# The last attention's softmax sums: folded to 128x8, inverted there, read back broadcast, and the product moved to GpSimd, with a new order of steps

## The reference

```python
q = (x @ Wq).reshape(b, n, 16, 64).transpose(0, 2, 1, 3) * 64 ** -0.5
kv = jnp.concatenate([jnp.broadcast_to(null_kv, (b, 1, 64)), x @ Wkv], axis=1)
sim = jnp.einsum('bhid,bjd->bhij', q, kv)
attn = softmax(where(causal_mask, mask_value, sim))
out = jnp.einsum('bhij,bjd->bhid', attn, kv)
return out.transpose(0, 2, 1, 3).reshape(b, n, 1024) @ Wout
```

## Time and profile before

| | us |
|---|---|
| median of 3 runs | 2005.79 (2002.66 to 2008.48) |
| profiled execution | 2003.36 |
| its span, first to last instruction | 2001.0 |
| last attention in it, jobs and close | about 1430 to 1930 |

### The profile page before, as it was taken

One profiled execution on the slowest core, in us unless ns is written; L12 is line 12 of the kernel. 1 busy time (PEld: TensorE's weight loads), 2 busy tenths in 40 slices (PEclk: granted clock), 3 DMA queues, 4 the chain that ended last, 5 costly groups with the idle time before them and its releaser, 6 DMA issues.

```text
span 2001.0 us, 31764 instructions
## 1 busy us (share of the span) xinstructions
PE 1849.8 (92%) x9960; PEld 1272.3 (64%) x9960; DVE 1399.3 (70%) x3825; ACT 964.6 (48%) x2008; POOL 1225.7 (61%) x1600
## 2 busy tenths in 40 slices
PE   5999999999895999999999999998999999899985
PEld 4566666666694666666676567887556665455554
DVE  8898888888344776766666456455788888776733
ACT  2544445545454455455455435444444444455443
POOL 1766788888553566776777700012467676799744
PEclk8999999999997899999999999999899999999998
DMA  5224233322344334344344120001322222222243
GB/s 149 67 70 114 68 94 95 79 57 60 89 142 114 84 84 98 86 110 95 88 101 98 42 88 22 1 13 30 82 57 57 65 68 60 65 77 70 56 117 98
DMA packets 125968, 155.57 MB, mean 78 GB/s; under 512 B 21880, under 2 KB 66200, under 8 KB 125544
## 3 DMA queue, kind: packets, MB, share of 16 engines
q1 hardware_dynamic: 121704, 145.42, 29.5%
q0 software_dynamic: 4096, 8.12, 1.2%
HBM read 47.84 MB, written 17.40 MB: 33 GB/s over the span
## 4 chain that ended last, share of the span: by engine, by line
PE 60%; DVE 14%; POOL 9%; issue 8%; ACT 3%; DMA 3%; SPq 3%; POOLq 0%; DVEq 0%; ACTq 0%
PE P L858 59%; POOL acc L1639 3%; POOL yd L1656 3%; DVE mx L2019 2%; DVE P L2030 2%; SPq L1760 1%; POOL acc L1636 1%; DMA qA<-hq 1%; POOL pr L1617 1%; POOL xg L1647 1%; DVE rd L2078 1%; DVE P L2077 1%; DVE z L2084 1%; PE P L957 1%; DVE mx L2040 0%
## 5 line engine op out<-in xcount | busy, mean ns | idle before, releaser
L1639 POOL TENSOR_TENSOR acc<-acc,pr 128x512 f32<-128x512 f32 (+3 forms) x768 | 677.3, 904 | 87.3 <-ACT pr L1398 63.0
L1398 ACT ACTIVATE pr<-P 128x512 f32<-128x512 f32 (+1 forms) x768 | 396.9, 568 | 331.4 <-PE P L858 288.0
L858 PE MATMUL P<-qA,kA 128*128 128x512 f32 (+2 forms) x1024 | 392.9, 387 | 17.1 <-ACT pr L1398 11.1
L858 PE MATMUL P<-pr,vt 128*64 128x512 f32 (+3 forms) x2304 | 403.3, 491 | 4.7 <-POOL pr L1617 4.5
L858 PE MATMUL P<-qB,kB 128*128 128x512 f32 (+2 forms) x1024 | 367.8, 365 | 0.0
L858 PE MATMUL P<-kA,qA 128*128 128x512 f32 (+2 forms) x1152 | 318.2, 376 | 30.5 <-DMA qA<-hq 9.3
L1617 POOL TENSOR_SCALAR_AFFINE_SELECT pr<-pr 128x256 f32<-128x256 f32 x384 | 156.5, 408 | 272.6 <-ACT pr L1398 215.7
L858 PEld LDWEIGHTS P<-pr,vt 128*64 128x64 f32 x2304 | 155.2, 137 | 217.3 <-issue 178.7
L2019 DVE TENSOR_REDUCE mx<-P 128x1 f32<-128x512 f32 x384 | 241.6, 683 | 30.8 <-PE P L858 29.0
L858 PEld LDWEIGHTS P<-qA,kA 128*128 128x128 f32 x1024 | 195.1, 191 | 102.8 <-ACT pr L1398 48.5
L858 PEld LDWEIGHTS P<-kA,qA 128*128 128x128 f32 x1152 | 193.7, 195 | 102.1 <-issue 25.8
(11 more groups left out here) (350 smaller groups left out, 2766.0 us busy)
## 6 DMA issues: line engine op xcount, KB each, us to landing
qA<-hq SPq DMA_DIRECT2D x384, 128.0 KB
kA<-stage SPq DMA_DIRECT2D x158, 128.0 KB, 2.3
qB<-qB SPq DMA_DIRECT2D x96, 128.0 KB, 2.5
kB<-stage SPq DMA_DIRECT2D x79, 128.0 KB
nr<-null_share SPq DMA_DIRECT2D x64, 128.0 KB, 3.0
yd<-in_c_zero SPq DMA_DIRECT2D x32, 128.0 KB, 2.7
w<-in_L_W SPq DMA_DIRECT2D x16, 256.0 KB, 5.0
xg<-xg SPq DMA_DIRECT2D x24, 129.0 KB
```

What stands on the lines that cost most here:

```text
L858: return P.matmul(out, lhs, rhs, start=start, stop=stop)
L1398: S.activation(a.pr[slot][:, r, 512 - wide:512], m.bank[b][:, 512 - wide:512], AF.Exp, scale=0.125).then_inc(s.free[b], 1)
L1639: G.tensor_tensor(acc[:, sl], acc[:, sl], pt[:, sl], ALU.add).then_inc(s.acc, 1)
```

## The change

Nothing changes in layers 0 to 2 but the way an index is written. In the last attention, for all chunks but the two of the last job (`at_once` is true for those, and for the other layers):

- The sums go another way. ACT copies the closed sums out of the bank into `rd` (`close`), which frees the bank. SP folds two partitions of `rd`, 1024 numbers, to 128x8 in `rc` (`fold`). DVE adds the null key's share, which now comes back as 128x8 in `nl` by one transfer, and takes the reciprocal, both at 128x8 (`recip`). SP writes the result to DRAM (`spread`) and reads it back broadcast over 64 partitions for each head into `rb` (`cast`). ACT copies the bank of `pv` to `z` (`zraw`), and POOL multiplies `z` by `rb` (`div`).
- `dsum`, the two ACT steps, the three DVE steps and the two broadcasts of `nr` go away there.
- The two heads' additions to `acc` become one instruction of twice the width.
- `STEPS[3]` is rewritten. `mxe` gets a step `X` of its own, later than `mxc`. A job has 16 `+`. The step `C1` stands behind the second `S` as before; `C0` moves from behind the seventh `S` to behind the ninth. The steps left over at the end are issued behind the last job.

```diff
-HELD = {"close": "div",  "q": "qlo", "k": "klo"}
+def at_once(L, b, p):
+    return L != 3 or (b, p) == (1, 7)
...
-    3: ("k0' + q0' S q0 k0 V3 + k0\" + R1 q0\" S + C1 + k1 + + S D1 S V3 + M2 + S M0 S k1' q1' q1 + S M1 + C0 "
-        "v0 + V k1\" + R0 q1\" D0 + v1 + M6 S + M3 M4 S M5 S M8 S S + M7 O1 O0 M9 +")}
+    3: ("q0 k0' + + k0 k1 q0' S k0\" V3 + R1 S q0\" + v0 F1 C1 S S + M1 M0 k1' S q1' q1 S + W1 + Z1 B1 q1\" M2 "
+        "I1 + + S v1 k1\" + V4 O0' M5 S + + F0 X0 M3 D1 S M6 C0 + R0 + M4 S M9 W0 I0 V4 + + M8 Z0 S M7 S D0 X1 "
+        "O1 B0")}
...
 ScalarE
+            elif kind == "close" and not at_once(*k[0:3]):
+                S.copy(a.rd[:], ps[:]).then_inc(s.free[b], 1)
+            elif kind == "zraw":
+                S.copy(a.z[pl.chunk(*k) % 4][:], m.bank[b][:]).then_inc(s.free[b], 1)
...
 GpSimd
-                        G.tensor_tensor(acc[:, sl], acc[:, sl], pt[:, sl], ALU.add).then_inc(s.acc, 1)
+                        G.tensor_tensor(acc[:, :, sl], acc[:, :, sl], pt[:, :, sl], ALU.add).then_inc(s.acc, 1)
+            elif kind == "div" and not at_once(*k[0:3]):
+                w.wait_ge(s.cast, 16 * od.nth("cast", *k))
+                G.tensor_tensor(z[:], z[:], a.rb[n][:], ALU.mult).then_inc(s.div, 1)
...
 SyncE
+                    src = nd[i].rearrange("i n -> (i n)").rearrange("(p e) -> p e", e=8)
+                    Y.dma_start(m.A[3].nl[i % 4][:], src).then_inc(s.n_in[i % 2], 16)
+            elif kind == "fold":
+                w.wait_ge(*pl.emptied("close", *k))
+                Y.dma_start(a.rc[n][:], a.rd[0:128:64, :].rearrange("r (p e) -> r p e", e=8)).then_inc(s.fold, 16)
+            elif kind == "spread":
+                w.wait_ge(s.recip, od.nth("recip", *k))
+                Y.dma_start(sd[...].rearrange("(p e) -> p e", e=8), m.A[k[0]].rc[n][:]).then_inc(s.spread, 16)
+            elif kind == "cast":
+                w.wait_ge(s.spread, 16 * od.nth("spread", *k))
+                Y.dma_start(a.rb[n][:], src).then_inc(s.cast, 16)
...
 VectorE
+            elif kind == "recip":
+                w.wait_ge(s.fold, 16 * od.nth("fold", *k))
+                    chain(V.tensor_tensor(a.rc[n][:], a.rc[n][:], a.nl[i % 4][:], ALU.add))
+                V.reciprocal(a.rc[n][:], a.rc[n][:]).then_inc(s.recip, 1)
```

More of the change, by code:

```diff
@@ L146, in add @@
                 turn.append(b)
-                if kind in HELD and len(got) == n - 1:
+                if kind in HELD and len(got) == n - 1 and (kind != "close" or at_once(*item[1:4])):
                     self.held[b] = (HELD[kind],) + item[1:]
@@ L196 @@
 SCORED = [(0, kt) for kt in range(4)] + [(1, kt) for kt in range(8)]
+SHARES_OUT = {"C": "close", "F": "fold", "I": "recip", "W": "spread", "B": "cast", "Z": "zraw", "D": "div", "O": "out"}
 STEPS = {
@@ L283, in step @@
             od.extend(project(L, "k", jobs[j + 1][0], keys(j + 1)[0], n)["'\"".find(what[-1]) + 1])
+        elif what[0] == "X" and at < 15:
+            od.add("mxe", L, *jobs[at + 1], int(what[1]))
         elif what[0] == "R":
@@ L289, in step, with finish @@
                     od.add("nrd", L, *jobs[at], n)
-        elif what[0] == "C" and done:
-            od.add("close", *done)
-            if L == 3:
-                od.add("dsum", *done)
-        elif what[0] == "D" and done:
-            od.add("div", *done)
-        elif what[0] == "O" and done:
-            if done[2] % 2:
-                if L == 3 and done == (3, 0, 1, 0):
-                    od.add("nbias", L)
-                od.add("out", *done)
+        elif what[0] in SHARES_OUT and done:
+            finish(SHARES_OUT[what[0]], done)
+    def finish(kind, done):
+        b, p = done[1:3]
+        if kind == "out":
+            if p % 2:
+                if done == (3, 0, 1, 0):
+                    od.add("nbias", 3)
+                od.add("out", *done)
+        elif not at_once(L, b, p):
+            od.add(kind, *done)
+        elif kind == "close":
+            od.extend([(x,) + done for x in ("close", "dsum", "yinv") if L == 3 or x != "dsum"])
+        elif kind == "div":
+            od.add("div", *done)
     scored = []
@@ L334, in attention_order @@
     od.extend([("pv", *k) for k in scored])
-    od.extend([(k, L, 1, 7, 1) for k in ("close", "dsum", "div", "out") if L == 3 or k != "dsum"])
+    left = [(L, *jobs[j], c) for j in range(13, 16) for c in range(2)]
+    for kind in SHARES_OUT.values():
+        for done in left:
+            if (kind,) + done not in od.place:
+                finish(kind, done)
     for items in behind:
@@ L609, in attention @@
         a.rd = sb(stack, "rd", [128, 512])
+        if L == 3:
+            a.rb = [sb(stack, f"rb{i}", [128, 512]) for i in range(2)]
+            a.rc = [sb(stack, f"rc{i}", [128, 8]) for i in range(2)]
         a.mx = [sb(stack, f"mx{i}", [128, 72]) for i in range(2)]
@@ L716, in signals @@
     s.w_hi, s.root, s.xn_a, s.x_hi = one("w_hi"), one("root"), one("xn_a"), one("x_hi")
-    s.q_hi, s.k_hi, s.inv = one("q_hi"), one("k_hi"), one("inv")
+    s.q_hi, s.k_hi, s.inv, s.recip, s.div = one("q_hi"), one("k_hi"), one("inv"), one("recip"), one("div")
+    s.fold, s.spread, s.cast = one("fold"), one("spread"), one("cast")
     s.rt_wh, s.rt_exp, s.xs, s.c_act, s.silu = one("rt_wh"), one("rt_exp"), one("xs"), one("c_act"), one("silu")
@@ L759, in __init__ @@
                 self.normed |= {(it[1], g): n for g in range(lo // 4, hi // 4)}
+        self.casts = [it[1:] for it in od.items if it[0] == "cast"]
+        self.closes = [it[1:] for it in od.items if it[0] == "close"]
+        self.n_div = {}
+        for it in od.items:
+            if it[0] == "div" and not at_once(*it[1:4]):
+                self.n_div[it[1:]] = len(self.n_div) + 1
         self.adds, n = {}, 0
@@ L784, in weighed, with cast_slot, close_before @@
     def weighed(self, L, b, p, c):
+        if not at_once(L, b, p):
+            return self.s.div, self.n_div[L, b, p, c]
         return self.emptied("pv", L, b, p, c, 0)
+    def cast_slot(self, a, *k):
+        casts = [x for x in self.casts if x[0] == k[0]]
+        i, n = casts.index(k), len(a.rb)
+        return i % n, casts[i - n] if i >= n else None
+    def close_before(self, *k):
+        i = self.closes.index(k)
+        return self.closes[i - 1] if i and self.closes[i - 1][0] == k[0] else None
     def keys_copied(self, n, second=False):
```

87 lines of the change are left out of this document (62 added, 25 removed).

## The result

The changed kernel took 2020.38 us in the median of 4 runs (2017.39 to 2024.72), against 2004.85 for the kernel before in the same comparison (2002.66 to 2008.48): a ratio of 1.008, 95% interval 1.0057 to 1.0103. It is slower, by 0.8%, and lies above the range that was predicted. Its profiled execution took 2017.39 us, with a span of 2015.6.

What follows compares the result with a forecast made beforehand. Bisection jobs were taken as bound by PE, scatter jobs by POOL, with PE idle 34.5 us in 500. From 2003.36: first routing job -2, bisection -2.6, slots -3, scatters +1, end 0, together -6.6, so 1997 us; range 1980 to 2012.

Steps and rivals of the forecast that it cites:

- The prediction's part on SP and the DMAs: New transfer chain from the sums' close to the product: 10 to 13 us with queueing, counted as costing nothing.
- Scatter jobs: Last-attention jobs with scatters, bound by POOL: stay at about 32.9 us, but fill 4.0 jobs rather than 3.6; counted +1.
- rival 2: Scatter jobs: merged additions save nothing, POOL waits about 1 us at one product of each pair; 2011 us, chance 0.14.
- First routing job: First last-attention job with routing, 35.5 us, DVE as its bound: -2 of PE's 3.3 us idle.
- Bisection jobs: Six last-attention jobs, 30.8 us each, bound by PE: half of their 5.2 us idle goes, -2.6.
- Slots and scatters together: Two jobs around the slots, stalled behind closings on DVE: -3 with a little clock; the jobs with scatters: +1.
- `X`: Exp of the null key's score, moved later: takes away ACT's 110.6 us of waits, counted at nothing beyond the idle shares.
- The number of `+`: 16 for 18 in a job: 8 scatters rather than 9, over 4.0 jobs rather than 3.6, +2 us.
- the middle course: DVE's relief in the last attention, allowing for longer waits at small steps: about 1 to 3 us a job.
- rival 3: Bisection jobs: DVE's small SBUF steps each wait for a merged POOL addition; about 2018 us, chance 0.09.
- The end: Last job, closed the old way: one POOL product more (+1.3), merged additions (-1.5), output moved; counted 0.
- Rival 1: Last attention: PE loses almost no time outside the scatter jobs and scatters cost nothing more; 1983 us, chance 0.18.

Runs made afterwards that it cites:

- e1: The changed kernel with the broadcast `cast` issued as two transfers, one a head with 64 partitions each, in place of one: 1986.2 us, ratio 0.9893.
- e12: e1 with the product by 1/sum on GpSimd in jobs up to the tenth and on VectorE from the tenth on: 1978.0 us, ratio 0.9851.
- e9: The kernel before with only the exp of the null key's score (`X`) moved to a later step of its own: 2009.83 us, ratio 1.0006.
- e6: e1 with the exp of the null key's score (`X`) put back directly behind the comparison: 2005.36 us, ratio 1.0003.
- e10: The kernel before with `X` moved later and the two heads' additions merged, old order and closing otherwise: 1994.48 us, ratio 0.9912.
- e4: The kernel before with only the two heads' additions in the last attention merged into one instruction: 2002.9 us, ratio 0.9967.
- e7: e1 with the two heads' additions as two instructions again: 1993.89 us, ratio 0.9943.
- e11: e1 with 18 `+` in a job, as in the kernel before, in place of 16: 2019.71 us, ratio 1.0045.
- e3: The kernel before with its two broadcasts of `nr` made into one transfer of outermost dimension 2: 2011.34 us, ratio 1.0016.

## Why the prediction was wrong

**The broadcast, the step that failed.** The prediction's part on SP and the DMAs took `cast` at 3.0 to 3.3 us, from two broadcasts of 64 partitions and a load of 256 KB, and went from size alone. It measured 8.24 and 8.62 where it stood on the chain. The rows it leant on were of broadcasts with an outermost dimension of 64. The line that builds `src`, the first one of e1's diff, has a 2 there and stood in the changed kernel to be read. With 3.0 us the chain came to 10 to 13, and "there POOL may stand for 0 to 3 us" was then closed with "POOL is behind PE, so the cast has landed. Nothing, then." With 5 more, 25 products wait for 2.9 each, and copies and scatters come late with them. This one term is what separates the changed kernel from e1: 34 us. The small transfers of the chain were over-priced, but that did not help: writing the inverted sums to DRAM landed in 1.4 us in the median, for 2.0 to 3.0.

**Without that step** the forecast of 1997 would still have been 11 us too high: e1 takes 1986.2 (by its ratio, on the 2004.85 of the first comparison, 1983). So the whole size, the right sign included, hung on one transfer. The terms, by e1:

- Scatter jobs: forecast four at 32 to 33, in e1 33.2 each over three (99.68 / 3), and the neighbours that hold the rest at 30.5 and 29.8. Right. So rival 2 had the place and the engine. But its 1 us of waiting for each pair is not there in e1 (5.1 us in all), and in the changed kernel it is far more, in nearly all jobs, and from a cause that the rival did not name.
- First routing job: forecast -2, in e1 -2.1. Right.
- Bisection jobs: forecast -2.6 over six, "bound by PE", with 5.2 us in all to win. In e1 they win 9.2 (175.5 for 184.7). The step that failed is the floor: PE's busy time was read as work that can't shrink. The six jobs of e1:

```profile
1491.25:1666.74 175.49, 173.80 (x950) 113.92 (x951) 131.88 (x434) 87.97 (x195) 137.80 (x127) 1.00 0.30 70
```

  PE is busy 173.8 us for 179.5 before, at the full clock in both. A part of that may be moved work, as these jobs hold 96 items of the bisection in place of 108. From the last layer's weights to the end of the span the work is the same, 3243 matmuls recorded, and busy time shrinks there too, in the kernel before and then in e1:

```profile
1307.64:2001.00 693.36, 621.61 (x3243) 411.73 (x3241) 487.45 (x1413) 320.34 (x700) 427.47 (x551) 0.96 0.25 66
```
```profile
1311.02:1985.50 674.48, 611.03 (x3243) 412.59 (x3241) 424.35 (x1353) 318.01 (x700) 440.69 (x405) 0.95 0.27 68
```

  The profile models the ends of matmuls, so a stretch with matmuls queued in it reads as busy. In the bisection jobs the idle time was no ceiling; over the whole layer the best run, e12, wins 28.7 us (693.4 - 664.7), less than the 34.5 of idle time.
- Slots and scatters together: forecast -3 and +1. In e1 -8.8 (219.1 for 227.9 in the marks 8 to 15). No run takes the two apart. The two jobs at 33.8 and 38.0, at a clock of 0.95 and 0.91, have no like in e1: the jobs around its slots take 29.2 and 30.5 at the full clock. The clock's share, counted as "a little", is by an estimate at most 5 of these 12 us (0.05 x 33.8 + 0.09 x 38.0); the rest is not taken apart.
- `X`, counted "at nothing": right in the old order (e9, 1.0006), and worth 19 us of medians in the new one (e6 against e1, 2005.36 - 1986.2). In the old order it is worth 8 us as soon as the additions are merged (e10 against e4). So ACT's 110.6 us of waiting cost nothing only while something else was late; that this was GpSimd's additions is argued, not shown.
- The merged additions: an instruction of 1024 takes 2380 ns for two of 1281, as worked out, and the saving of 1.5 a job was bounded well. Yet alone they are worth 6 us (e4), and 8 in e1 (e7). Over 16 jobs 1.5 would be 24; it shows where POOL binds.
- The number of `+`: treated as a question of how many jobs hold scatters, +2 us for having fewer. Measured, 18 in place of 16 cost 33.5 us in the new order (e11), at the two places tried. Fewer is far better here, for a reason that was not foreseen; the term had the wrong sign and was too small by a factor of ten and more.
- VectorE. The groups of the changed kernel in 1430 to 1930 (busy, mean ns, idle before), with POOL's:

```profile
L1701 POOL TENSOR_TENSOR acc<-acc,pr 128x1024 f32<-128x1024 f32 x47 | 111.9, 2380 | 20.2 <-ACT pr L1444 17.4
...
L1707 POOL TENSOR_TENSOR z<-z,rb 128x512 f32<-128x512 f32 x30 | 38.3, 1275 | 72.5 <-DMA rb<-sum_share 72.4
...
L2132 DVE TENSOR_TENSOR mx<-mx,sn 128x8 fp32r<-128x8 f32 x29 | 22.7, 784 | 1.0
...
L2133 DVE TENSOR_TENSOR mx<-sn,mx 128x8 f32<-128x8 f32 x29 | 17.9, 617 | 1.0
...
L2167 DVE TENSOR_TENSOR rc<-rc,nl 128x8 f32<-128x8 f32 x30 | 16.6, 554 | 13.2 <-DMA rc<-rd 13.1
L2168 DVE RECIPROCAL rc<-rc 128x8 f32<-128x8 f32 x30 | 6.1, 203 | 1.0
```

The new addition takes 554 ns (0.7 was taken), the reciprocal 203 (170). The comparisons are at 784 and 617 ns, for 708 and 667 before: the first is longer, the second shorter, the two together 1.40 us for 1.38. The runs that merge or part the additions alone say the same: 1.38 before and 1.25 with them merged (e4), 1.25 parted (e7) and 1.23 merged (e1). The longest grow: 1.42 and 1.75 us in e1, 0.99 and 1.20 in e7. The new addition has such tails too, as its durations show (min, median and max, first and last start):

```profile
L2167 DVE TENSOR_TENSOR rc<-rc,nl x30: 153/302/2048, 1438.2 to 1916.4; 128x8 f32<-128x8 f32 x30
```

The rule on the shared port that the prediction weighed (the Trainium skill, "SBUF — State Buffer", section "Who interferes with whom") would let the waits grow with GpSimd's instructions; the traces bear out the tails, and show no growth of the mean. So DVE won 2.8 - 0.55 - 0.20 = 2.0 us a chunk, the full relief and not the middle course, and rival 3 had no ground. In the six bisection jobs DVE is busy 20.5 to 24.3 us each, where 22 to 25.5 were forecast, and this relief did not carry the changed kernel below 30.8 a job.

**The end** was counted at 0, and moved by +0.9 in the changed kernel and -1.9 in e1, all at VectorE's addition (26.2, 25.3 and 23.4). Ahead of the first closing the new order loses 6.4 to 6.7 us, of which 4.2 come back up to mark 1; the sum had no term for that.

**One reading** of the profile was off: in the slices 29 to 38 VectorE is at 6 to 8 tenths, not 7 to 8. Nothing rested on it.

**The rivals, then.** Rival 1, all of PE's idle time won, at 1983, is nearly what e1 does, and e12 goes below it. The result itself belongs to none of the four. By the number rival 3 is nearest, at 2018, but that is luck, since its mechanism is absent. By the mechanism it is rival 2, with POOL waiting at a product, but its price of 1 us a pair came from no row, and the row that would have priced it did not exist in the kernel before. What could have been read was the form of the transfer in the diff. The chance of slower, 0.23, was not small; the range ended 8 us too low.

What stays open: why `X` and the merged additions win more together than the sum of each (e4, e9, e10), why 18 items cost so much in every second job, and what the new closing itself is worth, since e10 does almost as well without it and no run has e1 without it in an order that suits the old closing.

## What to carry to other kernels

Price a transfer by its outermost dimension as well as by its size: a broadcast written as 2 x 64 x 512 ran at a DMA share of 2 in 16 engines, and cutting it in two halves of 64 partitions was worth 34 us of 2020 here. The same form cost next to nothing where no engine stood waiting for it (e3), so read who waits, and what is queued behind the one that waits. Where an engine is the bound in one stage and not in the next, let the work go to the engine with slack in each stage (e12), and don't take PE's busy time for a floor.
